# Dispatching twelve of sixteen sequences to their experts during the attention before, in a fused two-layer kernel

## What is computed

```python
x = _layernorm(x + _L0_attn_ref(x, ...))   # gated long convolution
x = _layernorm(x + _L0_ffn_ref(x, ...))    # latent attention, then 7 routed SwiGLU experts and a shared one
x = _layernorm(x + _L1_attn_ref(x, ...))   # 16 heads of 8, causal, with biases
x = _layernorm(x + _L1_ffn_ref(x, ...))    # 8 experts, the 2 best per token
```

```python
gate_probs = softmax(x @ Wg + bg)                     # Wg 128 x 8
_, top_idx = top_k(gate_probs, 2)
selected = gate_probs * one_hot(top_idx).sum(-2)
selected = selected / (selected.sum(-1) + 1e-8)
h = gelu(einsum('bsf,efh->bseh', x, W1) + b1)         # W1 8 x 128 x 512
expert_out = einsum('bseh,ehf->bsef', h, W2) + b2     # W2 8 x 512 x 128
return einsum('bsef,bse->bsf', expert_out, selected)
```

## Time and profile before

| | |
|---|---|
| Median of 3 runs | 2999.65 us (2990.07 to 3002.31) |
| Profiled execution | 2997.73 us |
| its span, first to last instruction | 2996.0 us |
| granted TensorE clock, mean | 0.923 of full speed |
| busy: PE, DVE, ACT, POOL | 2461.2, 2129.1, 1439.5, 1338.7 us |
| DMA | 229.7 MB, mean 77 GB/s |

### The profile page before, as it was taken

The page is one execution under the profiler, slowest core; times in us unless marked ns, Lnnn a source line. Parts: engine busy times, 40 slices in busy tenths (PEclk is TensorE's granted clock), DMA queues, the critical chain, the costliest instruction groups (busy, mean ns, idle before and its releaser), DMA issues. The chain is left out here.

```text
span 2996.0 us, 49367 instructions
## 1 busy us (share of the span) xinstructions
PE 2461.2 (82%) x15431; PEld 1749.2 (58%) x15431; DVE 2129.1 (71%) x8106; ACT 1439.5 (48%) x2603; POOL 1338.7 (45%) x2609
## 2 busy tenths in 40 slices
PE   4558857999999999488888489999999975989981
PEld 3326745666666666276666366666666645877761
DVE  6537746887877876288888467777777746668684
ACT  3103313666666666122222146666666642877860
POOL 4520023555555554222222135655665544771176
PEclk9989977999999999599999779999999995999995
DMA  3260012322322321211110122221221307787762
GB/s 50 85 217 25 22 14 31 48 44 35 52 36 43 48 33 31 91 59 53 53 38 17 24 38 33 45 39 30 45 42 27 44 14 271 251 264 246 245 211 71
DMA packets 198796, 229.72 MB, mean 77 GB/s; under 512 B 48621, under 2 KB 148814, under 8 KB 190478
## 3 DMA queue, kind: packets, MB, share of 16 engines
q1 hardware_dynamic: 184482, 204.48, 28.1%
q0 software_dynamic: 8192, 16.79, 1.7%
q10 hardware_dynamic: 5868, 5.31, 0.8%
HBM read 132.55 MB, written 58.10 MB: 64 GB/s over the span
## 5 line engine op out<-in xcount | busy, mean ns | idle before, releaser
L1498 PE MATMUL banks<-Kb,Qb 96*128 96x512 f32 (+3 forms) x2048 | 616.2, 349 | 54.7 <-issue 37.1
L1507 PE MATMUL banks<-Qb,Kb 98*128 98x512 f32 (+1 forms) x1408 | 573.8, 413 | 27.7 <-ACT mha_prob L1396 16.3
L1168 DVE CUSTOM_DVE_ANT_0 mha_junk<-banks,mha_mask 128x512 bf16<-128x512 f32 (+3 forms) x1024 | 453.6, 488 | 187.8 <-PE banks L1498 175.4
L1168 DVE CUSTOM_DVE_ANT_0 mla_junk<-banks,mla_mask 128x512 bf16<-128x512 f32 (+3 forms) x1024 | 454.3, 488 | 157.7 <-PE banks L1498 138.9
L1498 PEld LDWEIGHTS banks<-Kb,Qb 96*128 96x128 f32 x2048 | 372.5, 196 | 300.5 <-DVE mha_nm L1168 100.0
L1396 ACT ACTIVATE mla_prob<-banks 128x512 f32<-128x512 f32 (+1 forms) x704 | 374.9, 559 | 270.0 <-PE banks L1507 268.9
L1396 ACT ACTIVATE mha_prob<-banks 128x512 f32<-128x512 f32 (+1 forms) x704 | 372.6, 559 | 243.2 <-PE banks L1507 239.7
L1291 POOL TENSOR_SCALAR_AFFINE_SELECT mla_prob<-mla_prob 128x128 f32<-128x128 f32 (+2 forms) x704 | 236.6, 347 | 287.9 <-PEq L1506 279.1
L1291 POOL TENSOR_SCALAR_AFFINE_SELECT mha_prob<-mha_prob 128x128 f32<-128x128 f32 (+2 forms) x704 | 237.7, 346 | 268.3 <-PEq L1506 257.2
L1507 PEld LDWEIGHTS banks<-Qb,Kb 98*128 98x128 f32 x1408 | 270.1, 193 | 115.6 <-issue 96.9
L1883 ACT ACTIVATE glu_sg<-banks 128x512 f32<-128x512 f32 x128 | 76.4, 597 | 259.3 <-PE banks L1897 259.3
(11 more groups left out here) (439 smaller groups left out, 5115.6 us busy)
## 6 DMA issues: line engine op xcount, KB each, us to landing
moe_wt<-expert_rows SPq DMA_DIRECT2D x53, 1024.0 KB, 5.1
conv_tz<-conv_kernel SPq DMA_DIRECT2D x16, 1024.0 KB, 7.6
moe_xg<-slots SPq DMA_DIRECT2D x53, 256.0 KB, 5.5
results<-moe_yt SPq DMA_DIRECT2D x53, 256.0 KB, 2.6
Qb<-mla_qh SPq DMA_DIRECT2D x128, 64.0 KB
Qb<-mha_qh SPq DMA_DIRECT2D x128, 64.0 KB
expert_rows<-moe_wt SPq DMA_DIRECT2D x8, 1024.0 KB, 8.4
Kb<-mla_kh SPq DMA_DIRECT2D x30, 256.0 KB, 6.0
```

Of the source, the lines that this page charges most:

```text
L1168: last = dve.tensor_tensor_reduce(junk[:, k % 3, at:at + w], ps[:, bank1(k), at:at + w], mask[:, L - w:L], -1.0, BIG, ALU.add, ALU.min, nm ...
L1498: last = pe.matmul(ps[:, bank1(k), at:at + w], Qb[0:MROW, u, g, h, j * P:(j + 1) * P], Kb[0:MROW, u, g, 0:w], start=True, stop=True)
L1507: pe.matmul(ps[:, bank2(g, k), 0:WIDE[k]].rearrange("p (x w) -> p x w", x=heads), Kb[0:MROW + 2, u, grp, kb * P:(kb + 1) * P], Qb[0:MROW + ...
```

## The change

Routing and scattering of sequences 0 to 11 move into the second attention, three and four sequences behind the one in work. Each expert now has a fixed region of 12 tiles for them, plus 7 spare tiles, so that slots can be given before the totals are known; at the end `tiles` turns the totals into a list of tiles (`place`, the region's tile, and `own`, the expert), which SP reads per tile. The last stage routes only sequences 12 to 15. There are two groups, of 31 and 15 tiles, 46 for 53. The area to clear is 3840 rows per sequence for 2048. The split of the expert weights moves into the shared experts: per tile 2 to 9 one expert, ACT for the high and POOL for the low part; the biases are packed behind the weights in one row. Combinations stand 1.25 tiles apart for 1.6. The weights of the latent attention stay in SBUF, and the tables of the dispatch lie on top of them. The diff, cut to its core:

```diff
@@ constants, and a class that holds what lives across stages
+SENT = 12
+SPARE = E1 - 1
+ROUTED = E1 * SENT + SPARE
-CLEAR = 4 * L
+CLEAR = 30 * P
+WROW = 4 * H1
@@ attention_stage
+        ROUTE = dict(pe=(1, 7), act=(1, 8), logits=(1, 11), dve=((2, 1), (2, 3), (2, 6), (2, 8), (3, 1), (3, 6)),
+                     counts=(2, 11), pool=(10, 11), tiles=(0, 6))
+        ROUTED_AT, SENT_AT = 3, 4
+        def routes(n):
+            return not latent and 0 <= n - ROUTED_AT < SENT
@@ sync
                 queries(0)
+                if not latent:
+                    sp.dma_start(D.wr, experts["Wg"]).then_inc(route_consts, 16)
+                    sp.dma_start(D.rb, rows(experts["bg"])).then_inc(route_consts, 16)
+                    sp.dma_start(tri, io["c_tri"]).then_inc(route_consts, 16)
@@ vector: in slots, and the steps
+                            if routes(n) and at in ROUTE["dve"]:
+                                route(n - ROUTED_AT, ROUTE["dve"].index(at))
+                            if not latent and n == SENT + ROUTED_AT and at == ROUTE["tiles"]:
+                                tiles()
...
+                    def highest(p, m):
+                        link(dve.tensor_reduce(m, p, axis=AX.X, op=ALU.max))
+                        link(dve.tensor_tensor(eq, p, each(m), ALU.is_equal))
+                        link(dve.tensor_tensor(eq, eq, over(D.desc), ALU.mult))
+                    def chosen(sel):
+                        link(dve.tensor_reduce(den, eq, axis=AX.X, op=ALU.max))
+                        link(dve.tensor_tensor(sel, over(D.desc), each(den), ALU.is_equal))
+                    def place(a, sel):
+                        link(dve.tensor_tensor(eq, sel, pos, ALU.mult))
+                        link(dve.tensor_reduce(den, eq, axis=AX.X, op=ALU.add))
+                        link(dve.tensor_copy(D.slot[:, a, r * BLK:(r + 1) * BLK], den))
+                    if step == 0:
+                        dve.wait_ge(rl_ready, c.next(rl_ready))
+                        link(dve.tensor_tensor(lg, ps[:, MB, 0:BLK * E1].rearrange("p (t e) -> p t e", e=E1),
+                                               over(D.rb), ALU.add))
+                        dve.sem_inc(mb_free, 1)
+                        highest(lg, m1)
+                    if step == 1:
+                        chosen(s1)
+                        dve.tensor_tensor(pr, lg, each(m1), ALU.subtract)
+                        link(dve.scalar_tensor_tensor(ex, s1, NEG, lg, ALU.mult, ALU.add))
+                    if step == 2:
+                        highest(ex, m2)
+                        chosen(s2)
+                    if step == 3:
+                        link(dve.tensor_tensor(took[:, :, :], s1, s2, ALU.add))
+                        link(dve.tensor_copy(run[:, 0, :], run[:, BLK, :]))
+                        for b in range(BLK):
+                            link(dve.tensor_tensor(run[:, b + 1, :], run[:, b, :], took[:, b, :], ALU.add))
+                        dve.sem_inc(took_ready, 1)
+                    if step == 4:
+                        dve.wait_ge(count_ready, c.next(count_ready))
...
+                        dve.sem_inc(mb_free, 1)
+                        place(0, s1)
+                    if step == 5:
+                        place(1, s2)
+                        dve.sem_inc(slot_ready, 1)
@@ gpsimd
+                            if not latent and 0 <= n - SENT_AT < SENT and k in ROUTE["pool"]:
+                                scatter(n - SENT_AT, g, ROUTE["pool"].index(k))
+                def scatter(r, b, a):
...
+                    pool.indirect_dma_start(D.slots, bass.IndirectOffsetOnAxis(D.slot[:, a, t:t + 1], 0),
+                                            X[:, r, b, :], None).then_inc(D.scattered, 16)
@@ scalar
+                            if routes(n) and at == ROUTE["act"]:
+                                act.wait_ge(rt_ready, c.next(rt_ready))
+                                act.activation(ctxt[:, :], ps[:, MA, :], ACT.Copy).then_inc(xr_ready, 1)
@@ tensor: at (1, 7), (1, 11) and (2, 11)
+                def route_transpose(r):
+                    pe.wait_ge(ma_free, c.next(ma_free))
+                    for b in range(BLK):
+                        last = pe.transpose(ps[:, MA, b * P:(b + 1) * P], X[:, r, b, :], ident[:, :])
+                def route_logits():
+                    pe.wait_ge(xr_ready, c.next(xr_ready))
...
+                    pe.wait_ge(mb_free, c.next(mb_free))
+                    for b in range(BLK):
+                        last = pe.matmul(ps[:, MB, b * E1:(b + 1) * E1], ctxt[:, b * P:(b + 1) * P], D.wr, ...
+                def route_counts(total):
+                    pe.wait_ge(took_ready, c.next(took_ready))
+                    pe.wait_ge(mb_free, c.next(mb_free))
...
@@ swiglu_experts_stage, sync
+        LOADED, HIGH_AT, LOW_AT, STORED = 3, 2, 3, 5
+                for n in range(NB):
+                    load(n, n % 2)
+                    sp.dma_start(D.slots[n * CLEAR:(n + 1) * CLEAR, :]..., io["c_zero"]).then_inc(D.cleared, 16)
...
+                    if 0 <= n - STORED < E1:
+                        store_expert(n - STORED)
+                    if 0 <= n - LOADED < E1:
+                        load_expert(n - LOADED)
@@ swiglu_experts_stage, gpsimd at the tile's end; scalar at e == 5
+                    pool.tensor_tensor(w[:, W1L:W1L + H1], x[:, 0:H1], f32(w[:, W1H:W1H + H1]), ALU.subtract)
+                    pool.tensor_tensor(w[:, W2L:W2L + H1], x[:, H1:2 * H1], f32(w[:, W2H:W2H + H1]), ALU.subtract)
+                    act.activation(w[:, W1H:W1H + H1], x[:, 0:H1], ACT.Copy)
+                    act.activation(w[:, W2H:W2H + H1], x[:, H1:2 * H1], ACT.Copy).then_inc(high_ready, 1)
@@ gelu_experts_stage
-        GROUPS = ((0, 4), (4, 8), (12, 4))
+        GROUPS = ((0, SENT), (SENT, NB - SENT))
+        COUNT, PLACE, GATES, MOVE = 1, (0, 2), ((2, 1), (3, 1)), (4, 1)
-                g = FIRST[q + 1] + 4 + (8 * j + 4) // 5 if q + 1 < len(GROUPS) else ALL
+                g = FIRST[q + 1] + 4 + (5 * j + 2) // 4 if q + 1 < len(GROUPS) else ALL
@@ sync: constants, then
+                sp.wait_ge(D.scattered, SENT * BLK * 2 * 16)
...
+                        src = slots_t[sp.value_load(D.place[0:1, g:g + 1], min_val=0, max_val=ROUTED - 1)]
...
-                    sp.dma_start(f32(wt[:, g % WBUFS, :]), wd[e]).then_inc(w_in[g % WBUFS], 16)
-                    sp.dma_start(bt[:, g % WBUFS, :], biases[:, e, :]).then_inc(w_in[g % WBUFS], 16)
+                    sp.dma_start(f32(wt[:, g % WBUFS, :]), D.rows[e]).then_inc(w_in[g % WBUFS], 16)
@@ vector
-                for e in range(RAWS):
-                    weights(e)
-                for q in range(len(GROUPS)):
-                    route(q)
-                    positions(q)
...
+                route()
                 low_x(0)
...
+                        if g == 0 and m in PLACE:
+                            (positions, send)[PLACE.index(m)]()
+                        if (g, m) in GATES:
+                            gates(GATES.index((g, m)))
+                        if (g, m) == MOVE:
+                            back()
@@ gpsimd
-                for q, (first, n) in enumerate(GROUPS):
-                    pool.wait_ge(slot_ready, c.next(slot_ready))
-                    for j in range(n):
+                pool.wait_ge(slot_ready, c.next(slot_ready))
+                for j in range(LAST):
@@ scalar, tensor
-                for s in range(NB):
+                for s in range(LAST):
```

446 lines of the change are left out of this document (260 added, 186 removed).

## The result

The changed kernel takes 3011.3 us (median of nine runs, 2994.3 to 3016.6) against 2998.0 us for the kernel before (nine runs, 2979.3 to 3002.3): ratio 1.0048, 95% interval 1.0030 to 1.0065. The prediction was 2972 us with a range of 2936 to 3004 and a chance of 0.72 for faster. The kernel came out 13 us slower where 26 us faster was forecast, and the range doesn't hold the result. By the prediction's own measure (15 us can't be told from no change) this is "the same", to which it gave 0.19. Two of its signs of being wrong stood at an attention longer by over 80 us and shared experts longer by over 12; the first was met (81.4), the second nearly (11.6). The profiled execution of the changed kernel took 3004.3 us (span 3002.6).

A forecast was written before the change was run, and what follows sets the result against it. VectorE bounds the shared experts, TensorE the second attention, first tile's start and POOL's gathers the last stage. Last stage minus 81, attention plus 52, shared experts plus 3: minus 26 from 2997.7 us, so 2972 us, range 2936 to 3004.

The forecast's parts named there:

- signs of being wrong: Attention longer by under 30 or over 80 us, tail over 215, or shared experts longer by over 12.
- The bound of each stage: VectorE holds shared experts, TensorE the second attention; in the last stage, first tile's start and POOL's gather chain count.
- every part of the last stage: Last stage: front minus 59.4 us, loop minus 58.5, tail plus 37.3; in all minus 81 us.
- the place and size of the waits in the attention: Second attention: 1.25 us per sequence for VectorE in quarter 2, 1.5 us for POOL before the transposes.
- the work added to TensorE: Second attention: transposes, logits, count products and refilling, 1.6 us for each of twelve sequences, 19 us (17 to 26).
- the scatters at 1.0 us: Second attention: scatters beside VectorE take 1.0 us each.
- held by TensorE (692 of 731 us, 95%, at the full 2.4 GHz level): Second attention: TensorE bounds it, so a microsecond of TensorE there costs a microsecond; attention plus 52 us (20 to 95).
- all four rivals: Attention absorbs it, 0.22; VectorE's routing half exposed or first tile not advanced, together 0.19; POOL becomes the bound, 0.09.
- the tile owners: Second attention, once: making the tile owners on VectorE costs 2 us.
- VectorE, which bounds, gets nothing: Shared experts: weight rows add work to ACT and POOL but none to VectorE; plus 3 us (0 to 12).
- Half exposed: Second attention: VectorE's routing costs 2.9 us per sequence in place of 1.25, 2992 us; 0.19 together with the late first tile.
- the late first tile: Last stage: weight rows come slowly, front shrinks by only 40 us, 2992 us; 0.19 together with Half exposed.

The follow-up runs named there:

- e6: The kernel before, unchanged, profiled on a chip other than the first: 3135.3 us.
- e11: Kernel before plus 19 unread small VectorE operations per sequence in quarters 0 and 1 of the second attention: 3150.6 us, ratio to before 1.0029.
- e7: Changed kernel with the edits of e2 and e4, VectorE's routing steps spread wider, scatters a quarter later, tile owners moved: 2989.4 us, ratio to before 0.953.
- e9: e7 with the last 32 scatters paced eight at a time and POOL's subtractions cut into four pieces each: 2967.8 us, ratio to before 0.944.
- e10: e7 without the making of the weight rows (ACT's copies and POOL's subtractions left out; loads, stores, clears kept): 2990.3 us.
- e3: Changed kernel with the edits of both e1 and e2: 3007.5 us, ratio to before 0.959.
- e2: Changed kernel with POOL's signal to the next sequence's transposes given after the second of four preparations: 3008.9 us, ratio to before 0.960.
- e8: Kernel before plus 19 unread small VectorE operations per sequence in quarter 2 of the second attention: 3186.8 us, ratio to before 1.015.
- e1: Changed kernel with VectorE's routing steps 1 to 5 and the counts moved to later places, out of quarter 2: 3028.3 us, ratio to before 0.967.
- e5: The changed kernel as it is, on a chip other than the first: 3035.0 us, ratio to before 0.969.
- e4: Changed kernel with the first of POOL's two subtractions per shared-expert tile moved ahead of the gates' power: 3034.1 us.

## Why the prediction was wrong

**Right.** The bound of each stage, every part of the last stage (minus 79.3 for minus 81), the place and size of the waits in the attention, the work added to TensorE, and the scatters at 1.0 us. At the full clock a sequence with routing is 4.4 us longer, as predicted, and the twelve together 51 us where 49 were predicted.

**The step that failed** is the one ahead of the sum: the second attention was taken as "held by TensorE (692 of 731 us, 95%, at the full 2.4 GHz level)", and every later microsecond was priced at that level. The level was not a given of the stage. In the kernel before it held, with TensorE idle for 1.65 us of each 44.2. In the changed one TensorE is idle for 2.3 us more, works on small products in between, and the clock falls. A term for that was missing in the sum, in the bounds (20 to 95 held the result only by luck) and in all four rivals. It cost 16.5 us in the twelve sequences, by the periods, and is part of the 6.3 us behind them. With it two terms failed that have nothing to do with the routed sequences: the tile owners, put at 2 us, took 3.7 on VectorE and a wait of 3.4 with a fall behind it, and the drain at the stage's end, put at nothing, took 7.9 us more. 51 + 16.5 + 6.3 + 7.9 - 0.3 = 81.4 stand against 49 + 3.

The clock loss by run, with TensorE's idle time per sequence at the full clock (period less busy time), and divided by what stands right ahead of each fall:

| kernel | idle per sequence | clock loss in the walk | of it behind waits for helpers | behind the logit products | at the tile owners' wait |
|---|---|---|---|---|---|
| before; e6 | 1.65 us | 0; 0 | 0 | 0 | 0 |
| e11 | 1.84 us | 1.7 us | 1.7 | none there | none there |
| e7; e9; e10 | 1.4 to 1.8 us | 6.8; 10.2; 10.2 us | 0; 0; 0 | 3.4; 3.4; 3.4 | 3.4; 6.8; 6.8 |
| e3 | 2.5 to 2.8 us | 15.3 us | 1.7 | 6.8 | 6.8 |
| e2 | 3.1 us | 25.6 us | 6.8 | 15.4 | 3.4 |
| e8 | 3.5 us | 23.8 us | 23.8 | none there | none there |
| e1 | 3.8 us | 28.9 us | 8.5 | 17.0 | 3.4 |
| changed kernel; e5; e4 | 3.9 to 4.1 us | 28.9; 37.4; 27.2 us | 17.0; 30.6; 13.6 | 8.5; 3.4; 6.8 | 3.4; 3.4; 6.8 |

Where a fall comes varies between runs of one kernel: the nine runs of the changed kernel have mean clocks of 0.911 to 0.920, the slowest (3016.6 us) the lowest and the fastest (2994.3) the highest. But the groups stand apart: three profiles of the changed kernel's attention lose 27 to 37 us, three of e7's 7 to 10, two of the kernel before nothing. Where the added waits for helpers are gone (e7, e9, e10), what is left is one fall behind the logit products and one at the tile owners, for which TensorE waits 2.9 us in one piece. That the products bring the clock down is read from where the falls stand, 2 to 3 us behind them in all nine kernels that have them; no run took them away, so this part is not shown.

**The smaller miss** is "VectorE, which bounds, gets nothing" in the shared experts. The prediction named the shared port, but weighed it only for scatters beside VectorE, not for POOL's new subtractions beside VectorE's small operations. 0.92 us x 8 = 7 us, 15 us of clock loss against 3.4, of which VectorE, the bound of that stage, passes on a part, and 2.4 us for clears and transfers (e10); 11.6 in place of 3 in all. How much of it the falls and ACT's copies take was not tried. This was the place where the rule that the prediction cites did bear.

**Among the rivals** none was it. "Half exposed" and the late first tile have the nearest time (2992), both by the wrong mechanism. From the forecast of 2972 to the profiled 3004.3: 29.4 in the attention, 8.6 in the shared experts, 1.7 in the last stage, less 7.1 ahead of the shared experts, which the change doesn't touch and which lies within what that stretch varies by (1221.7 to 1230.5 us over these runs).

## What to carry to other kernels

Where TensorE paces a stage at its full clock, price a new wait twice: once as itself and once for the clock it may bring down. Here 2.3 us of short waits per sequence cost 28 us in twelve sequences, and the falls 16.5 us more on the first chip, some 26 in e5 and 22 in e8. Moving the same work to places where nobody waits returned 54 to 60 of 91 us. Work that comes only once can cost as much as its own length in one long wait (the tile owners). Look at the end of a stage that gets its first scatters, too: 7.9 us of drain stood in no sum. Put work that is added to a helper where that helper is idle, not where its data come ready, and look at what stands behind it in each queue (e1 moved a wait from VectorE to POOL). And time a change that removes scatters on more than one chip.

## What the runs showed of the hardware

- The granted clock falls to 1.2 GHz in sequences in which no gap of TensorE is longer than 1.0 us (0.8 us in e8). (The Trainium skill, TensorE: Matmul & The Clock Gate, A second HAM failure mode: psum-queue depth-cycling, tells of such oscillation through frequent small gaps, without a size. The trace agrees for e8, whose three falls, 23.8 us of clock loss in a stage of 831 us, all stand behind such gaps.)
- A drain of POOL at the end of a stage in which it had scattered took 8.56 us in nine profiles of nine (in the changed kernel's with no transfer running), and 0.70 us in the four whose attention has no scatter.
- While POOL scatters, transfers of other queues can slow down, and by how much differs between the chips: in one and the same window the DMA moved 274 GB/s on one, 58 on another, with the scatters at the same 1.0 us. The same kernel took 2998 and 3136 us.
- VectorE's 0.18 us addition took up to 1.28 us beside a POOL subtraction, and its end stands 0.04 us from the subtraction's (1415.15 and 1415.11).
